# Transformer decoder stack on one core: the by-key products of the older unit ahead of the mask and scores of the newer one

## The reference

```python
x = x + _L0_attn_ref(_layernorm(x), ...)    # 16 heads of 16, causal
x = x + _L0_xattn_ref(_layernorm(x), ...)   # long convolution with the context
x = x + _L0_ffn_ref(_layernorm(x), ...)     # 2 shared and 16 routed experts
x = x + _L1_attn_ref(_layernorm(x), ...)    # 16 heads of 16, causal
x = x + _L1_xattn_ref(_layernorm(x), ctx_2048, ...)   # 32 heads of 8, padding masks
x = x + _L1_ffn_ref(_layernorm(x), ...)     # 32 routed experts, capacity bound
# each attention:
scores = jnp.einsum('bhqd,bhkd->bhqk', q, k) / math.sqrt(Dh)
attn = jax.nn.softmax(jnp.where(mask, scores, -jnp.inf), axis=-1)
out = jnp.einsum('bhqk,bhkd->bhqd', attn, v)
```

## Time and profile before

| | |
|---|---|
| timed runs | 663.7, 670.08, 672.96 us; median 670.08 us |
| the profiled execution's own time | 667.44 us |
| its span, first to last instruction | 665.7 us |
| PE busy | 582.2 us, 87% of the span |
| DVE busy | 367.1 us, 55% |
| POOL busy | 304.7 us, 46% |
| ACT busy | 259.7 us, 39% |
| mean granted TensorE clock | 0.941 of full |

### The profile page before, as it was taken

How to read it: one execution, slowest core, us unless ns; L and a number is a source line. 1 busy time by engine, 2 the same in 40 slices (tenths; PEclk the granted TensorE clock), 3 DMA queues, 4 the chain that set the end, 5 groups by cost and what they waited for, 6 DMA issues and landing times. The chain is left out here.

```text
span 665.7 us, 14122 instructions
## 1 busy us (share of the span) xinstructions
PE 582.2 (87%) x5411; PEld 365.7 (55%) x5411; DVE 367.1 (55%) x825; ACT 259.7 (39%) x544; POOL 304.7 (46%) x384
## 2 busy tenths in 40 slices
PE   4979999998599999999764698768999987899898
PEld 3435666544356666656542365535656656356577
DVE  3435665899545564534752656446676742954241
ACT  1213552100565666634441254514555543304340
POOL 2508752989645453310350576449788843300000
PEclk8888999999599999999998789979999989899999
DMA  6199418000025323313019985011130030004711
GB/s 242 63 159 176 176 56 348 1 0 1 0 69 164 107 96 102 105 60 104 4 36 175 117 131 194 9 33 41 45 101 2 4 143 2 1 0 163 265 35 63
DMA packets 32995, 59.81 MB, mean 90 GB/s; under 512 B 4011, under 2 KB 24509, under 8 KB 30881
## 3 DMA queue, kind: packets, MB, share of 16 engines
q1 hardware_dynamic: 32069, 56.65, 31.2%
q10 hardware_dynamic: 860, 2.26, 1.0%
HBM read 50.95 MB, written 6.63 MB: 86 GB/s over the span
## 5 line engine op out<-in xcount | busy, mean ns | idle before, releaser
L1275 PE MATMUL PS<-R 128*128 128x256 f16 (+6 forms) x2072 | 205.5, 268 | 5.2 <-DVE R L1145 3.2
L1275 PEld LDWEIGHTS PS<-R 128*128 128x128 f16 (+5 forms) x2072 | 133.2, 104 | 87.6 <-issue 51.6
L1068 DVE TENSOR_REDUCE mx<-PS 128x4 bf16<-128x512 f32 x128 | 82.4, 686 | 53.8 <-PE PS L1275 42.5
L774 ACT ACTIVATE R<-PS 128x512 f32<-128x512 f32 x128 | 69.5, 595 | 90.9 <-PE PS L1275 90.9
L565 POOL TENSOR_TENSOR R<-mx,causal 128x512 bf16<-128x512 bf16 x64 | 65.4, 1043 | 68.2 <-DVE mx L1068 52.9
L1275 PE MATMUL PS<-xnT,R 128*128 128x512 f16 (+1 forms) x348 | 85.1, 385 | 1.4 <-ACT xnT L687 1.4
L565 POOL TENSOR_TENSOR R<-mx,R 128x512 bf16<-128x512 bf16 x64 | 65.6, 1047 | 23.4 <-PE PS L1275 12.9
L1136 DVE TENSOR_TENSOR R<-R,wr 128x512 f32<-128x512 f32 (+1 forms) x46 | 33.9, 737 | 59.0 <-ACT R L852 59.0
L852 ACT ACTIVATE R<-PS,small 128x512 f32<-128x512 f32 (+1 forms) x50 | 34.3, 687 | 57.7 <-PE PS L1275 57.7
L1275 PEld LDWEIGHTS PS<-xnT,R 128*128 128x128 f16 (+1 forms) x348 | 34.3, 100 | 33.4 <-issue 2.5
L516 POOL TENSOR_SCALAR veps<-mv 128x1 f32<-128x1 f32 (+1 forms) x30 | 7.2, 240 | 89.0 <-DVE mv L936 88.9
(11 more groups left out here) (194 smaller groups left out, 843.5 us busy)
## 6 DMA issues: line engine op xcount, KB each, us to landing
R<-in_experts_dram SPq DMA_DIRECT2D x6, 1536.0 KB, 9.3
R<-qk_scr SPq DMA_DIRECT2D x48, 128.0 KB, 6.2
qk_scr<-R SPq DMA_DIRECT2D x16, 256.0 KB, 4.2
wr<-g_scr SPq DMA_DIRECT2D x16, 256.0 KB, 3.3
R<-in_w_dram SPq DMA_DIRECT2D x1, 3200.0 KB, 18.5
R<-in_w_dram SPq DMA_DIRECT2D x1, 3168.0 KB, 11.3
R<-in_toe_dram SPq DMA_DIRECT2D x1, 2048.0 KB, 15.8
wr<-g_scr SPq DMA_DIRECT2D x10, 192.0 KB, 2.8
```

The costliest lines, as they stand in the source:

```text
L774: s.activation(PTm[:, n % 4, 4 * k:4 * k + 4, :], bank(2 + (2 * n + k) % 3).rearrange("p (h q) -> p h q", h=4), ACT.Exp, scale=c["sc"]).th ...
L1068: v.tensor_reduce(mx[:, n % 4, 4 * k:4 * k + 4], bank(k).rearrange("p (h k) -> p h k", h=4), AX.X, ALU.max).then_inc(S("att_mx"), 1)
L1275: return nc.tensor.matmul(o_, l, r, start=start, stop=stop)
```

## The change

In the program of PE the block of lag 2 (`less_max`, `scores_by_key`) is put ahead of the block of lag 0 (`mask`, `scores`) in every step. Nothing else is touched.

```diff
                 for t in steps(run, 17):
+
+                    c, u = unit_at(run, t, 2)
+                    if c:
+                        less_max(c, u)
+                        scores_by_key(c, u)
                     c, u = unit_at(run, t, 0)
                     if c:
                         mask(c, u)
                         scores(c, u)
-                    c, u = unit_at(run, t, 2)
-                    if c:
-                        less_max(c, u)
-                        scores_by_key(c, u)
```

## The result

The changed kernel took 686.58 us (median of 4 runs, 681.39 to 687.76), the kernel before, in the same comparison, 669.54 (4 runs, 663.70 to 672.96). The ratio is 1.025, with an interval of 1.016 to 1.034: slower, by 17 us, where 8 were forecast. The time lies 0.6 us above the range.

A forecast was written before the change was run, and what follows sets the result against it. PE was taken to bound the kernel, full in plain steps and waiting at turns. Later turns 6.8, gain -0.85 and clock 2.0 made +8 us on 667.44: 675.5 us, with an 8-in-10 range of 666 to 686.

The forecast's parts named there:

- the direct cost of a turn: In steps where a batch is turned: PE waits up to 0.89 us longer for the low half at each affected turn.
- By so much the scores now start later: In every step, scores start 0.89 us later after the step's beginning, and with them maxima and LM.
- the low half comes 0.89 later: In batch steps the low half waits behind LM on POOL with nothing to cover it, so it comes 0.89 us later.
- Step 16: At its turn PE's wait of 1.82 us grows by 0.89 to 2.71, with a granted clock of 0.50 after it.
- Plain steps: Steps without a turn stay at 2.58 us and cost nothing, as 0.6 us of cover is left for LM.
- the head of the chain: In turn steps, scores of step t head one closed chain: scores, maxima, LM, low half, turn.
- The sum is 6.8: Later turns at steps 16, 26, 28, 30 and four of CROSS: 0.89 + 1.78 + 0.55 + 3.56 us; 3 to 9 possible.
- I take 2.0: Behind step 16's longer wait the clock falls to half speed and costs 2.0 us; bounds 0 and 4.
- The case that the clock falls more often: Rival: half clock follows three more waits, at step 26 and CROSS's turns, besides step 16; 682 us, chance 0.15.
- the three waits up to 1.58: Argument against more clock falls: turns waiting for R in the kernel before lie where turns ran at their usual 0.38.
- I take half, -0.85: At the starts of SELF0 and SELF1, filled mask waits gain 1.7 us; half is counted, as PE's later stop may absorb it.
- 675.5: Forecast time in us for the whole kernel: +8 on the profiled execution's 667.44; given chance 0.55.

The follow-up runs named there:

- e3: New order only in the steps where a turn is fed, the order of the kernel before in all others; 682.93 us, ratio 1.023.
- e2: Changed kernel with the old order put back only in the steps where a turn is fed; 676.11 us, ratio 1.009.
- e4: Changed kernel with matmuls whose results nothing uses filling PE's waits ahead of turns, steps 16 to 52; 680.03 us, ratio 1.017.
- e6: New order in steps 0 to 5 of both runs of attentions alone, later steps as in the kernel before; 669.95 us, ratio 1.002.
- e1: The kernel before run once more with no edit, to measure chance between executions; 668.65 us, ratio 0.998.
- e5: New order in the steps of CROSS alone, the order of the kernel before in SELF0 and SELF1; 682.99 us, ratio 1.012.
- e7: Kernel before with POOL's low half moved ahead of LM and ACT's high half ahead of the exponentials; 661.78 us, ratio 0.982.
- e9: Kernel before with only the low half moved ahead of LM on POOL, ACT's order left as it was; 664.58 us, ratio 0.988.
- e10: Kernel before with low and high halves moved ahead on POOL and ACT, and the last weights' conversion four steps later; 659.59 us, ratio 0.979.
- e8: Changed kernel with the low half moved ahead of LM on POOL and the high half ahead of the exponentials on ACT; 669.90 us, ratio 0.990.

## Why the prediction was wrong, point by point

**Right: the direct cost of a turn.** "By so much the scores now start later" and "the low half comes 0.89 later" hold within 0.03: 0.88, 0.87, 0.88 and 0.86 at CROSS's four turns. Step 16 was to wait 2.71 and waits 2.70. The half clock behind it came, too, as 0.77 and 0.66 over 6 us, against 1.00 in the earlier trace rows, but it cost 1.1 us up to the next turn (6.38 for 5.30) where 2.0 were forecast. Plain steps cost nothing, as forecast.

**Half right: the head of the chain.** The prediction said that the scores of the step that feeds the turn stand at its head. They stand at the head of one. A second of the same length starts two steps ahead of the turn and goes over the normalised rows. e3 delays only the first, e2 only the second, and in CROSS each pays nearly the full price, 0.73 and 0.86 a batch in e3 and 0.88 in e2. The mechanism was right for the changed kernel, where both are late, and would have been wrong for an edit that spares the one.

**Wrong in size: the term of the direct cost, by a little.** "The sum is 6.8" had 5.9 in this stretch (1.78, 0.55 and 3.56). Here e4 shows 7.0 as an upper bound: 3.3 up to step 30 (forecast 2.3), 1.1 to step 40 (0.89) and 2.6 in the three batches (2.67). Turn by turn e4 falls behind by 0.30, 0.87, 0.90 and 1.19 us at steps 24, 26, 28 and 30, where 0, 0.89, 0.89 and 0.55 were forecast. The surplus at steps 24 and 30 can be the filler's. At step 24 the wait went from 1.58 to 1.94, but that is no lateness: the turn stands 9.23 us behind CROSS's first mask and stood 9.89 behind it. What the longer wait did cost is the clock behind it.

**Wrong: the clock, the largest error.** "I take 2.0" counted one fall, behind step 16. The case that the clock falls more often was priced at 682 and given 0.15, because of the three waits up to 1.58 that had not lowered it. It is what happened, with 5.1 us in CROSS by the two traces and 6.5 over the whole kernel by the timed runs (686.58 less 680.03). The step that failed is the reading that waits shorter than the 1.82 of step 16 are safe. After step 16 the clock fell behind four more turns, with waits of 1.94, 1.48, 1.25 and 1.39. The length of a wait alone does not decide it in this range: 1.24 cost nothing at 513.07, and in e2 the clock stayed at 1.00 behind a wait of 2.05 at step 16.

**Wrong in part: the gain.** For "I take half, -0.85" the traces show some 0.5 us at SELF1's start (31.67 to 31.19), and the timed runs of e6 can show neither (1.002, 0.996 to 1.007). The way there was wrong: the masks' waits fell by 1.4 us in total, not by 3, and the longest grew from 2.5 to 2.9. The prediction saw that VectorE's piece slips behind the scores, but took 0.4 for it; it slips by 1.28. That what was gained could end in the stop of PE was foreseen, and the stop is 0.8 longer in this trace.

**The sum.** 675.5 was 667.44 + 8. With the measured terms it is 667.4 + 7.0 + 5.1 in this stretch, 0.9 for step 16's wait and about 1 for the clock behind it. That is 681.4. With the 2.85 us of chance up to SELF1 it is 684.3. What is left of 687.65, some 3 us, lies near 400 us, in a stop of PE without a releaser (0.8) and the half clock behind it (2.6), less the 0.5 gained. The row of the kernel after that answers to the last of the earlier trace rows:

```profile
404.52 0.93 PE L1275 MATMUL PS<-negidb,R 128*128 128x128 bf16 x7 [2.49 <-issue]
```

It was 1.67 before, and a half clock follows it now (0.51 from 403.7 to 410.6). Whether the change lengthens it is **open**. It took from 1.67 to 3.60 with the old order there (1.67, 1.94, 2.23, 3.41, 2.15, 1.67 and 3.60 in before, e1, e3, e5, e7, e9 and e10), 2.51 with the new one in steps 0 to 5 alone (e6), and 2.49, 3.04, 1.63 and 3.00 with the new one there (after, e2, e4, e8). That is no pattern; it wasn't tried apart from the transfers beside it. A half clock behind the stop came with the old order, too (0.59 from 414 to 416 us in e5).

Also open is why two of four turns with equal waits lose the clock. e4 shows that without this idle time the clock stays up there, not what decides among equal waits.

## What to carry to other kernels

When the engine that bounds the kernel is full, exchanging groups on it adds nothing and removes nothing, but it sets when every other engine's chain starts. Look for the places where such a chain ends in a wait that is already above zero, and follow all the chains that end there: two of one length can hide each other, so that undoing one brings nothing at that place. Where a short operation that someone waits for stands behind a long one that nobody waits for in another engine's queue, exchange those first; here that brought 1.8% where the exchange on PE lost 2.5%. And where a change lengthens waits of TensorE, price the clock that it can lose behind them, too: here waits from 1.24 to 1.94 us lost it in some places and kept it in others.

## What was not expected of the hardware

The granted clock fell to 1.2 GHz after a single wait of 1.25 us, with PE busy for 3.45 of the 4.70 us around it, and adding matmuls made the kernel 6.5 us faster (686.58 to 680.03). From CROSS's first mask on, the longest idle time of PE up to the turn of step 52 was 1.94 us, and the time at half clock there grew from about 5 to about 24 us (by the mean clocks: 0.91 over 29.90 us before; 0.75 over 35.03 and 0.92 over 41.16 after).

The Trainium skill, in "TensorE: Matmul & The Clock Gate", Part 1, ties the half clock to an idle window and puts the ramp at under 1% of a typical kernel's span. The trace of e4 agrees that idle time brings it on (0.98 in CROSS with the waits filled, 0.89 without). The falls that the filling took away are 1.0% of this kernel's time. But the kernel before, run once more (e1), shows a fall with no idle time at all (windows of e1):

```profile
286.00:290.00 4.00, 4.00 (x22) 1.90 (x19) 1.42 (x3) 1.51 (x3) 1.49 (x2) 1.00 0.30 109
...
294.00:295.90 1.90, 1.90 (x11) 0.97 (x10) 0.26 (x1) 0.00 (x0) 0.00 (x0) 1.00 0.28 104
295.90:299.30 3.40, 3.40 (x9) 1.05 (x9) 0.00 (x0) 0.00 (x0) 0.00 (x0) 0.50 0.01 5
```

PE is busy throughout. What it did from 286.9 to 295.6 was in good part f32 products with a matrix of 18 rows, 0.69 us for each pair, and at 295.9 the clock is halved for 3.4 us. The first execution did the same work at 1.00. So the clock can fall with no idle time ahead of it, and whether such a place loses the clock differs between executions of one program. Whether the 18 rows have to do with it was not tried.

PE also stops somewhere between 396 and 415 us in every trace, for 1.6 to 3.6 us, with nothing in the profile that it waits for, while transfers take 0.89 of the DMA engines' time around it in the kernel after (403.7 to 410.6 us). It differs by up to 2.0 us from one trace to the next, more than two turns of this change cost.
